# Turning the feed-forward x in place on VectorE, with its blocks regrouped through DRAM

## The chip, the cores and the metric

One core of one Trainium2 chip runs the whole program. The metric is device time in microseconds, the median of several executions. The engines are TensorE (matrix products; PE in the profile), VectorE (DVE), ScalarE (ACT), GpSimd (POOL) and SyncE (SP), which issues the DMAs here. Each engine works through its own instruction list in order and waits on semaphores.

## The reference

The input x has 8192 tokens of 512 numbers (8192x512, f32). What is computed:

```
mod = silu(c) @ wmod                       -> sa, ca, ga, sb, cb, gb   (512 each; ga, gb kept at least 0.25 from 0)
h = layernorm(x) * (1 + ca) + sa
x = x + ga * (causal linear attention of h, 16 heads of 32, then @ W_out + b_out)
h = layernorm(x) * (1 + cb) + sb
g = h @ (w_gate/127).T ;  u = h @ (w_up/127).T          (1536 hidden units)
x = x + gb * ((silu(g) * u) @ (w_down/127).T)
```

The weights w_gate, w_up and w_down are integers from -127 to 127. The result must be accurate to f32, so each f32 operand is split into a rounded high part and a low remainder (float32r), and products are taken with both.

## The kernel before, in words

The program has two parts that follow each other. The attention part takes 16 groups of 512 tokens. The feed-forward part takes 8 groups of 1024 tokens (FG = 8; group G, token tiles of 128, halves of 512 tokens) and runs from about 1012 us to the end. Its loop over G is written once in a hardware loop for the middle groups, and once each for the first and the last.

**Steps.** The hidden units are taken in 12 blocks of 128 (HB = 12; block q). For each block TensorE computes gate and up for both token halves with a Winograd scheme of seven products, p1 to p7, each of four matmuls 128x512 (`product`, line 1868). A step on TensorE is p1(q), p7(q-1), p2(q), p5(q), p4(q-1), p6(q), p3(q). The other engines work beside it:

- ACT (`step` in `scalar`) saves PSUM banks and takes the silu: save_p1 (line 1573), save_p5 (1568), silu1 (1583), h_high (1595), save_u2 (1578), h_high, then a place for something extra, silu2 (1590).
- VectorE (`step` in `vector`) adds and multiplies: add_c22(q-1) (line 1715), add_c11(q) (1704), times_gate2(q-1) (1729), times_gate1(q-1) (1721), a place for something extra (`aside`), add_c12(q) (1710).
- GpSimd computes the low parts of the hidden values, h_low (line 1497), and adds the residual (1502).

The waits around this are: p6(q) for add_c11(q), p5(q) for add_c12(q-1), p4(q-1) for add_c22(q-1), p7(q) for save_u2(q), which is behind silu1(q) on ACT; silu1(q) waits for times_gate1(q-1), and that for p4(q-1).

**Down rows.** After steps 5 and 11 comes a half of the down projection: eight token tiles (`down`, line 1925), each twelve matmuls, into four PSUM banks in turn. VectorE multiplies each by gb (`gate_y`, line 1736), GpSimd adds the residual that SP has loaded (`load_residual`, line 1411), SP stores it (`store`, 1428). A bank's next row waits for the gate_y of the row four before.

**The next group's x.** While group G runs, the tiles of group G+1 (loaded by `load_x`, line 1405, into eight tiles of 128x512: the four of xg and four of z_exp and z_relu) get their layer norm on VectorE: `norm_stats` (1681) in steps 2 to 5, `norm_var` in step 5, `rstd_of` on GpSimd, `norm_x` (1697) behind the first half and in steps 7 to 9. They have tokens on the partitions, and the products need features there. So TensorE turns them: `turn` (line 1936) makes four 128x128 transposes into a PSUM bank, eight times a group: behind steps 8 to 11, and four between the first down rows of the second half. ACT brings each bank to SBUF with scale and shift, `evacuate` (line 1562), one each in the extra place of steps 9 to 11, one after step 11 and four later.

**Behind step 11** VectorE makes the operands of the next group's products from these: the Winograd sums T1 to T4 (`sum_of`, 1671) and low parts (`low`, 1675) for both k, with ACT's high parts (`high`, 1547) between, and the second half's gate_y among them in a fixed order that ends with add_c11 of the next group, for which p6 of the next group waits:

```python
            sum_of(G + 1, T1, 0)
            sum_of(G + 1, T2, 0)
            add_c22(G, 11)
            sum_of(G + 1, T3, 0)
            times_gate2(G, 11)
            low(G + 1, T1, 0)
            times_gate1(G, 11)
```

**The SP queue** issues, in order, the loads of the weight parts for block q+4 (`load_parts`, line 1393, 1 MB, each waiting for p4 of the block that used its place), and after each six of them the stores and residual loads of a half; `load_x` stands among the second half's.

**End of the attention part.** The first feed-forward group's x is turned in the attention part. Its two halves are loaded into xg by one DMA each (line 404) in the last two attention groups; VectorE's `norm_stats` there (line 757) waits for them, and stands ahead of the gating and dividing of the attention tiles, for which TensorE waits.

Of the kernel before, what the change touches and what calls it, by code (L numbers as in the profile page):

```python
# [43 lines left out]
Shared = namedtuple("Shared", "xg xf h_hi h_lo ring b_hi b_lo full wd silu_sum saved gate h y x_res gb_row pairs sums dn")  # L44
# [24 lines left out]
def build(nc, x, w_qkv, b_qkv, b_cols, w_out, b_out, c_vec, c_row, w_mod, w_mod_t, ffn_words, out):  # L69
    top = ExitStack()  # L70
    with top:
# [10 lines left out]
        k_dram = nc.dram_tensor("k_dram", (P, D), F32, kind="Internal").ap()  # L82
        gb_dram = nc.dram_tensor("gb_dram", (1, D), F32, kind="Internal").ap()
# [60 lines left out]
        ffn = feed_forward(sem, later, ident, mod_col, half_neg, norm, gb_dram, parts, att, shared, x_mid, out)  # L144
# [40 lines left out]
def attention(nc, s, sem, sbuf, psum, ident, gb_dram, mod_col, half_neg, w_hi, w_lo, xt_hi, xt_lo, ga_row,  # L185
# [5 lines left out]
    z_exp = sbuf(s, "z_exp", [P, 2, GN])  # L191
    z_relu = sbuf(s, "z_relu", [P, 2, GN])
# [40 lines left out]
    v_ready, ksum_ready, prod_ready, prod_turned = sem("v_ready"), sem("ksum_ready"), sem("prod_ready"), sem("prod_turned")  # L233
# [26 lines left out]
    shared = Shared([xg[:, t, :] for t in range(GT)] + [z[:, i, :] for z in (z_exp, z_relu) for i in range(2)],  # L260
# [42 lines left out]
    def sync(sp, first_loads):  # L303
# [449 lines left out]
    def vector(dve, sum_of, low):  # L753
        def norm_stats(g, tiles=range(GT)):
            wait(dve, x_in, 16 * (g + 1))
# [568 lines left out]
def feed_forward(sem, later, ident, mod_col, half_neg, norm, gb_dram, parts, att, shared, x_mid, out):  # L1324

    stats, mean_var, var_eps, rstd = norm[1:5]
    xg, xf, h_hi, h_lo, (blocks, filled), b_hi, b_lo, full, wd, total, saved, gate, h, y, x_res, gb_row, xs, sums, dn = shared
# [8 lines left out]
    xt_ps, xf_ready = sem("fxt_ps"), sem("fxf_ready")  # L1336
    gb_in, gb_chain, gb_done = sem("gb_in"), sem("gb_chain"), sem("gb_done")
# [50 lines left out]
    def sync(sp):  # L1388
# [7 lines left out]
        def load_x(G):  # L1396
            if isinstance(G, int) and G == 1:
                sp.wait_ge(att.xt_ps, (NG + 2) * C)
            else:
                wait(sp, xt_ps, (G - 1) * 8)  # L1400
# [83 lines left out]
    def gpsimd(pool):  # L1484
# [24 lines left out]
        def body(G):  # L1509
            ahead = not isinstance(G, int) or G + 1 < FG  # L1510
            for q in range(HB):
                if q not in (5, 11):
                    h_low(G, q, 1)
                    h_low(G, q, 0)
                if q == 5:
                    h_low(G, q, 1)
                    h_low(G, q, 0)
                    if ahead:
                        rstd_of(G + 1)
# [18 lines left out]
    def scalar(act):  # L1538
# [10 lines left out]
        def evacuate(G, i, bank):  # L1549

            k, which = divmod(i, 4)
            c = (k, k + 2, k, k + 2)[which]
            wait(act, xt_ps, G * 8 + (i - 7))
# [8 lines left out]
            act.activation(to, bank, ACT.Identity, bias=mod_col[:, SB, c:c + 1],  # L1562
# [47 lines left out]
        def body(G):  # L1610
# [12 lines left out]
            for q in range(7, HB):  # L1623
                step(G, q, (lambda i=q - 9: evacuate(G + 1, i, dn[i])) if ahead and q >= 9 else nothing)
# [4 lines left out]
            evacuate(G + 1, 3, dn[3])  # L1629
# [7 lines left out]
            for i, bank in ((4, sums[0]), (5, sums[1]), (6, xs[0]), (7, xs[1])):  # L1637
                evacuate(G + 1, i, bank)
# [20 lines left out]
    def vector(dve):  # L1659
# [39 lines left out]

        def add_c11(G, q):  # L1700
# [54 lines left out]
        def step(G, q, extra, last_tile):  # L1755
            add_c22(G, q - 1)
            if isinstance(G, int) and G == 0 and q == 1:
                last_tile()
            add_c11(G, q)
            times_gate2(G, q - 1)  # L1760
            times_gate1(G, q - 1)
            extra()
            add_c12(G, q)

        def body(G, last_tile):
            ahead = not isinstance(G, int) or G + 1 < FG

            def aside(q):
# [19 lines left out]
            times_gate1(G, 5)  # L1788
            for i in range(FT - 1):
# [271 lines left out]
```

## Time and profile before

| | |
|---|---|
| time, median of 3 runs (lowest, highest) | 1996.83 us (1996.74, 1998.13) |
| the profiled execution: its time | 1998.45 us |
| its span, first to last instruction | 1996.7 us |
| TensorE's mean granted clock, share of full | 0.998 |
| one group of the feed-forward part (1298.54 to 1423.20) | 124.7 us |

A row of a timeline gives the start, the time taken (of all instructions merged into it), the engine, the line of the kernel, the operation, output and inputs by tile name with their shape, and in brackets how long the engine stood before it and what released it. Some names are shared, since tiles are reused: `k_tok` and `kv_diag` are ACT's saved banks, `r_den` is c11 or c12, `bv_row` is c22, `y_rows` the gated hidden values, `sc`, `pj`, `num` and `state` PSUM banks, `full` and `xf` the turned x and its sums.

### The profile page before, as it was taken

The numbers are of one execution on the slowest core, as the hardware profiler recorded it, in microseconds if no ns is written. First come the engines' busy times: TensorE is split into PE (matmuls) and PEld (weight loads), VectorE is DVE, ScalarE is ACT, GpSimd is POOL, SyncE is SP. The second block draws the span as 40 slices with busy tenths as digits, with TensorE's granted clock in tenths as the row PEclk, the third lists the DMA queues.
The fourth block names the chain that finished last, engine by engine and source line by source line (L and its number), as shares of the span: only waits on it lengthen the run. The fifth ranks groups of instructions, "written<-read, shape, count | busy, mean of one in ns | idle before, by whom it ended". The sixth has DMA issues, their size and how long they took to land. (4 is left out here: it accounts for less than half of the span.)

```text
span 1996.7 us, 43856 instructions
## 1 busy us (share of the span) xinstructions
PE 1960.6 (98%) x16008; PEld 1591.9 (80%) x16008; DVE 1443.1 (72%) x2386; ACT 905.7 (45%) x1542; POOL 877.4 (44%) x718
## 2 busy tenths in 40 slices
PE   7999999999999999999899999999999999999999
PEld 4788888888888888887678888788888888888887
DVE  7977888878788878787865857658576585765744
ACT  5443444344444434443344535445354453544533
POOL 2533544444544444453334443444434444344444
PEclk9999999999999999999999999999999999999999
DMA  7223333444434434432575654656546565465553
GB/s 268 69 91 102 115 123 119 135 130 133 135 100 133 128 125 135 127 110 90 179 263 176 207 187 145 214 170 209 186 144 215 171 210 186 144 214 174 169 168 106
DMA packets 202521, 309.81 MB, mean 155 GB/s; under 512 B 16145, under 2 KB 72977, under 8 KB 202386
## 3 DMA queue, kind: packets, MB, share of 16 engines
q1 hardware_dynamic: 201858, 306.78, 48.1%
q8 instruction: 107, 1.75, 0.4%
q10 hardware_dynamic: 528, 1.05, 0.1%
q14 instruction: 28, 0.23, 0.0%
HBM read 225.19 MB, written 82.58 MB: 154 GB/s over the span
## 5 line engine op out<-in xcount | busy, mean ns | idle before, releaser
L1497 POOL TENSOR_TENSOR h_lo<-y_rows,h_hi 128x512 fp32r<-128x512 f32 x192 | 246.5, 1301 | 367.6 <-ACT h_hi L1595 367.6
L461 POOL TENSOR_TENSOR x_res<-y,x_res 128x512 f32<-128x512 f32 x64 | 86.6, 1353 | 294.0 <-DVE y L872 283.5
L851 DVE TENSOR_TENSOR probs<-sc,causal 128x512 f32<-128x512 f32 x256 | 158.5, 681 | 3.8 <-PE sc L1156 2.6
L612 ACT ACTIVATE z_exp<-pj,qk_neg 128x512 f32<-128x512 f32 x128 | 87.7, 686 | 161.5 <-PE pj L1137 158.0
L1137 PE MATMUL pj<-xt_hi,w_hi 128*128 128x512 f32 x512 | 145.9, 406 | 5.7 <-DVE a_t L861 4.7
L1925 PE MATMUL sc<-wd,h_hi 128*128 128x512 f32 x384 | 150.7, 392 | 0.0
L1925 PE MATMUL sc<-wd,h_lo 128*128 128x512 f32 x384 | 149.6, 389 | 0.0
L450 POOL TENSOR_TENSOR a_lo<-a_t,a_hi 128x512 fp32r<-128x512 f32 x60 | 82.2, 1370 | 144.8 <-ACT a_hi L626 144.8
L1137 PE MATMUL pj<-xt_lo,w_hi 128*128 128x512 f32 x512 | 138.1, 391 | 1.8 <-DVE xt_lo L789 1.8
L1137 PE MATMUL pj<-xt_hi,w_lo 128*128 128x512 f32 x512 | 138.1, 392 | 0.0
L1710 DVE TENSOR_TENSOR r_den<-pj,k_tok 128x512 f32<-128x512 f32 x96 | 66.3, 691 | 97.9 <-ACT k_tok L1578 52.2
L1595 ACT ACTIVATE h_hi<-y_rows 128x512 fp32r<-128x512 f32 x192 | 119.0, 620 | 24.9 <-DVE y_rows L1729 13.4
L1573 ACT ACTIVATE k_tok<-sc 128x512 f32<-128x512 f32 x96 | 56.2, 585 | 158.7 <-PE sc L1868 158.7
L445 POOL TENSOR_TENSOR prod<-k_sum,qt 128x512 f32<-128x512 f32 x64 | 94.1, 1471 | 61.4 <-DVE qt L797 42.5
L597 ACT ACTIVATE xf<-sc,mod_col 128x512 f32<-128x512 f32 x64 | 49.8, 778 | 152.7 <-PE sc L1097 152.7
L1137 PEld LDWEIGHTS pj<-xt_hi,w_hi 128*128 128x128 f32 x512 | 91.8, 189 | 33.1 <-DVE a_t L861 11.0
L1137 PEld LDWEIGHTS pj<-xt_lo,w_hi 128*128 128x128 f32 x512 | 96.2, 188 | 23.3 <-DVE xt_lo L789 2.2
L1568 ACT ACTIVATE kv_diag<-pj 128x512 f32<-128x512 f32 x96 | 57.4, 598 | 123.9 <-PE pj L1868 122.9
L1137 PEld LDWEIGHTS pj<-xt_hi,w_lo 128*128 128x128 f32 x512 | 96.7, 189 | 20.9
L1583 ACT ACTIVATE k_sum<-r_den 128x512 f32<-128x512 f32 x96 | 60.7, 632 | 107.7 <-DVE y_rows L1721 95.0
L1721 DVE TENSOR_TENSOR y_rows<-sc,k_sum 128x512 f32<-128x512 f32 x96 | 66.3, 691 | 55.6 <-PE sc L1868 55.6
L1715 DVE TENSOR_TENSOR bv_row<-sc,kv_diag 128x512 f32<-128x512 f32 x96 | 66.3, 691 | 54.8 <-PE sc L1868 54.8
(248 smaller groups left out, 5390.4 us busy)
## 6 DMA issues: line engine op xcount, KB each, us to landing
w_hi<-parts SPq DMA_DIRECT2D x48, 1024.0 KB, 5.4
w_lo<-parts SPq DMA_DIRECT2D x48, 1024.0 KB, 5.4
x_mid<-x_res SPq DMA_DIRECT2D x96, 256.0 KB, 2.8
x_res<-in_L_attn_x SPq DMA_DIRECT2D x64, 256.0 KB, 2.8
k_dram<-k_block SPq DMA_DIRECT2D x252, 64.0 KB
xg<-in_L_attn_x SPq DMA_DIRECT2D x15, 1024.0 KB, 7.4
x_res<-x_mid SPq DMA_DIRECT2D x60, 256.0 KB, 3.9
full<-x_mid SPq DMA_DIRECT2D x60, 256.0 KB, 3.7
```

The costliest lines, as they stand in the source:

```text
L445: pool.tensor_tensor(out=prod[:, c % 2, :], in0=k_sum[:, c % 2, :], in1=qt[parity][:, c, :], op=ALU.mult).then_inc(prod_ready, 1)
L450: pool.tensor_tensor(out=a_lo[:, :], in0=a_t[:, :], in1=a_hi[:, :].bitcast(F32), op=ALU.subtract).then_inc(a_lo_ready, 1)
L461: pool.tensor_tensor(out=x_res[:, slot, :], in0=y[:, :], in1=x_res[:, slot, :], op=ALU.add).then_inc(y_ready, 1)
L612: act.activation(z_exp[:, n % 2, :], pj[:, n % 2, :], ACT.Relu, bias=qk_neg[:, 1 - kind, c:c + 1], scale=-scale).then_inc(below_ready, 1)
L851: dve.tensor_tensor(out=probs[:, h, :].rearrange("p (c i) -> p c i", c=C), in0=sc[:, h, :].rearrange("p (c i) -> p c i", c=C), in1=causal[ ...
L1137: mm = pe.matmul(to, w[:, k, at:at + P], xt[:, k, :], start=(i == 0), stop=(i == len(passes) - 1))
L1497: pool.tensor_tensor(out=h_lo[b], in0=h[i], in1=h_hi[b].bitcast(F32), op=ALU.subtract).then_inc(h_lo_ready, 1)
L1595: act.activation(h_hi[q % 6 * 2 + i], h[i], ACT.Copy).then_inc(h_hi_ready, 1)
L1710: dve.tensor_tensor(out=c12, in0=sums[1], in1=s12, op=ALU.add).then_inc(c12_ready, 1)
L1715: dve.tensor_tensor(out=c22, in0=xs[q % 2], in1=s5, op=ALU.add).then_inc(c22_ready, 1)
L1721: dve.tensor_tensor(out=h[0], in0=xs[q % 2], in1=gate[0], op=ALU.mult).then_inc(h1_ready, 1)
L1925: mm = pe.matmul(dn[i % 4], as_(part[j * 2 + t // GT][:, rows]), as_(wd[half * 6 + j]), start=(j == 0 and part is h_hi), stop=(j == 5 and ...
```

## The change

- TensorE's `turn` is taken out, with its waits. In its place VectorE's `turn` transposes a 128x512 tile in place, in blocks of 32x32, which leaves features and tokens in the right order only within a block.
- The blocks are therefore put in place by DMA ahead of it: after the layer norm, `save_xn` stores a half's four tiles to DRAM (`xn_dram`), and `load_blocks` loads them back so that partition block h holds columns h*128 to h*128+127, 32 tokens each (four DMAs of 256 KB in pieces of 512 bytes).
- The eight transposes stand singly among VectorE's instructions of steps 10 and 11. ACT's `evacuate` reads the turned tiles from SBUF by a strided pattern instead of PSUM: evac 0 and 1 in step 11's extra place, 2 and 3 right behind, 4 to 7 where they were.
- `norm_stats` and `norm_var` move one step ahead (not for the first group), `norm_x` to behind the first half and between its gated rows. `rstd_of` moves with them.
- add_c22 of block 11 moves ahead of T1 and T2.
- Since features now come in another order (head slices regrouped), w_gate, w_up and the sb and cb rows of wmod are reordered on the host, and the two loads of line 404 become sixteen DMAs each, whose source pieces are 32 numbers (128 bytes).

```diff
+        z = sbuf(s, "z", [P, 4, GN])        # was z_exp and z_relu
...
-                sp.dma_start(xg[:, :, :], mid_groups[half, :, :, :]).then_inc(x_in, 16)
+                for t in range(GT):
+                    for c in range(C):
+                        sp.dma_start(xg[:, t, c * P:(c + 1) * P].rearrange("p (h e) -> p h e", h=HPC),
+                                     mid_groups[half, :, t, :].rearrange("p (h c e) -> c p h e", h=HPC, c=C)[c]
+                                     ).then_inc(x_in, 16)
...
+        def save_xn(G, second):
+            wait(sp, xn_ready, G * 4 + (2 * second - 2))
+            sp.dma_start(xn_dram[second * GN:(second + 1) * GN, :].rearrange("(t p) d -> p t d", p=P),
+                         xg_halves[second][:, :, :]).then_inc(xn_out[second], 16)
+
+        def load_blocks(G, second):
+            wait(sp, xn_out[second], G * 16)
+            for h in range(HPC):
+                sp.dma_start(xg_halves[second][h * E:(h + 1) * E, :, :].rearrange("p t (b x) -> p (t b) x", x=P),
+                             xn_dram[second * GN:(second + 1) * GN, h * P:(h + 1) * P].rearrange("(b i) x -> i b x", i=E)
+                             ).then_inc(xb_in[second], 16)
...
                     if not last or q + 4 < HB:
                         load_parts(G, q + 4)
+                    if not last and q in (5, 6):
+                        save_xn(G + 1, q - 5)
+                    if not last and q in (7, 8):
+                        load_blocks(G + 1, q - 7)
...
-        def evacuate(G, i, bank):
+        def evacuate(G, i):
...
-            wait(act, xt_ps, G * 8 + (i - 7))
+            c, second = (k, k + 2, k, k + 2)[which], which // 2
+            wait(act, xt_ps, G * 8 + (4 * second - 4))
...
-            act.activation(to, bank, ACT.Identity, bias=mod_col[:, SB, c:c + 1],
+            turned = xg_halves[second][:, :, :].rearrange("p t (b c i) -> p c (t b) i", c=C, i=E)[:, c, :, :]
+            act.activation(to.rearrange("p (b i) -> p b i", i=E), turned, ACT.Identity, bias=mod_col[:, SB, c:c + 1],
...
-                step(G, q, (lambda i=q - 9: evacuate(G + 1, i, dn[i])) if ahead and q >= 9 else nothing)
+                step(G, q, (lambda: (evacuate(G + 1, 0), evacuate(G + 1, 1))) if ahead and q == 11 else nothing)
...
-            evacuate(G + 1, 3, dn[3])
+            evacuate(G + 1, 2)
+            evacuate(G + 1, 3)
...
+        def turn(G, t):
+            wait(dve, xb_in[t // GT], G * (16 * HPC))
+            dve.transpose(xg[t], xg[t]).then_inc(xt_ps, 1)
...
             add_c22(G, q - 1)
...
+            turning = q >= 10 and (not isinstance(G, int) or G + 1 < FG)
+            first = (q - 10) * GT
+            if turning:
+                turn(G + 1, first)
             add_c11(G, q)
             times_gate2(G, q - 1)
+            if turning:
+                turn(G + 1, first + 1)
             times_gate1(G, q - 1)
             extra()
+            if turning:
+                turn(G + 1, first + 2)
             add_c12(G, q)
+            if turning:
+                turn(G + 1, first + 3)
...
-                if ahead and not first and 2 <= q < 6:
-                    norm_stats(G + 1, q - 2)
-                if ahead and q == 5:
+                if ahead and not first and 1 <= q < 5:
+                    norm_stats(G + 1, q - 1)
+                if ahead and q == (5 if first else 4):
                     norm_var(G + 1)
-                if ahead and 7 <= q < 10:
-                    norm_x(G + 1, q - 6)
...
             times_gate1(G, 5)
+            if ahead:
+                norm_x(G + 1, 0)
+                norm_x(G + 1, 1)
             for i in range(FT - 1):
                 gate_y(G, i)
+                if ahead and i in (3, 4):
+                    norm_x(G + 1, i - 1)
...
+            add_c22(G, 11)
             sum_of(G + 1, T1, 0)
             sum_of(G + 1, T2, 0)
-            add_c22(G, 11)
...
-        def turn(G, i, bank):
-            k, which = divmod(i, 4)
-            c, second = (k, k + 2, k, k + 2)[which], which // 2
-            wait(pe, xn_ready, G * 4 + (2 * second - 2))
-            for t in range(GT):
-                mm = pe.transpose(bank[:, t * P:(t + 1) * P], xg[second * GT + t][:, c * P:(c + 1) * P], ident[:, :])
-            mm.then_inc(xt_ps, 1)
```

## Rows read from the trace of the kernel before

**Rows 1.** Busy time, share of the span and instructions of TensorE, whole execution.

```profile
PE 1960.6 (98%) x16008; PEld 1591.9 (80%) x16008; DVE 1443.1 (72%) x2386; ACT 905.7 (45%) x1542; POOL 877.4 (44%) x718
```

**Rows 2.** Waits of TensorE's weight loads, 1012 to 1997: us in total, times, longest.

```profile
PEld sc L1868 <- ACT k_tok L1578: 12.1, 42, 0.7
PEld sc L1925 <- DVE a_t L1736: 1.5, 7, 0.2
```

**Rows 3.** Timeline of TensorE around the turn behind step 8.

```profile
1450.89 0.62 PE L1868 MATMUL pj<-xt_hi,w_hi 128*128 128x512 f32 x2
1451.35 0.60 PE L1936 MATMUL num<-ident,xg 128*128 128x128 f32 x4
1451.70 0.71 PE L1868 MATMUL sc<-w_hi,w_lo 128*128 128x512 f32 x2
1452.25 0.63 PE L1868 MATMUL sc<-xt_hi,w_lo 128*128 128x512 f32 x2
```

**Rows 4.** Timeline of VectorE: times_gate1(9), times_gate1(10), T1, T2, add_c22(11).

```profile
1463.50 0.69 DVE L1721 TENSOR_TENSOR y_rows<-sc,k_sum 128x512 f32<-128x512 f32 x1 [0.61 <-PE sc L1868]
...
1470.34 0.69 DVE L1721 TENSOR_TENSOR y_rows<-sc,k_sum 128x512 f32<-128x512 f32 x1 [0.61 <-PE sc L1868]
...
1473.98 1.47 DVE L1671 TENSOR_TENSOR full<-xf 128x512 f32<-128x512 f32 x1 [0.44 <-ACT xf L1562]
1475.49 0.69 DVE L1671 TENSOR_TENSOR full<-r_den,full 128x512 f32<-128x512 f32 x1
1476.10 0.68 DVE L1715 TENSOR_TENSOR bv_row<-sc,kv_diag 128x512 f32<-128x512 f32 x1
```

**Rows 5.** Timeline of all engines where the next group begins; then VectorE in its steps.

```profile
1499.84 0.68 DVE L1704 TENSOR_TENSOR r_den<-pj,k_tok 128x512 f32<-128x512 f32 x1
...
1500.64 0.30 PEld L1868 LDWEIGHTS sc<-w_lo,w_hi 128*128 128x128 f32 x2 [0.25 <-issue]
...
1513.90 0.69 DVE L1721 TENSOR_TENSOR y_rows<-sc,k_sum 128x512 f32<-128x512 f32 x1 [0.62 <-PE sc L1868]
...
1517.61 0.69 DVE L1715 TENSOR_TENSOR bv_row<-sc,kv_diag 128x512 f32<-128x512 f32 x1 [0.51 <-PE sc L1868]
...
1520.44 0.69 DVE L1721 TENSOR_TENSOR y_rows<-sc,k_sum 128x512 f32<-128x512 f32 x1 [0.62 <-PE sc L1868]
```

**Rows 6.** Timeline of ACT in step 11: evac 2 and silu2(11).

```profile
1473.18 0.77 ACT L1562 ACTIVATE xf<-sc,mod_col 128x512 f32<-128x512 f32 x1
1473.84 0.63 ACT L1590 ACTIVATE gabo_row<-r_den 128x512 f32<-128x512 f32 x1
```

**Rows 7.** Timeline of GpSimd: both h_low of block 10.

```profile
1472.35 2.55 POOL L1497 TENSOR_TENSOR h_lo<-y_rows,h_hi 128x512 fp32r<-128x512 f32 x2 [4.29 <-ACT h_hi L1595]
```

**Rows 8.** Line 845, attention's transposes on VectorE: min/median/max ns, first and last start.

```profile
L845 DVE STREAM_TRANSPOSE k_block<-kt x63: 662/670/714, 63.4 to 972.8; 128x512 f32<-128x512 f32 x63
```

**Rows 9.** Timeline of SP's issues: the two loads of line 404.

```profile
895.78 0.39 SPq L404 DMA_DIRECT2D xg<-x_mid  x1
...
956.47 0.39 SPq L404 DMA_DIRECT2D xg<-x_mid  x1
```

**Rows 10.** Timeline of VectorE, bn_stats of the first of these loads.

```profile
908.02 1.86 DVE L757 BATCH_NORM_STATS2 stats<-xg 128x6 f32<-128x512 f32 x3
```

**Rows 11.** Timeline of VectorE in the last attention group, from the second bn_stats.

```profile
962.17 1.29 DVE L757 BATCH_NORM_STATS2 stats<-xg 128x6 f32<-128x512 f32 x2 [0.45 <-DMA xg<-x_mid]
963.63 0.69 DVE L872 TENSOR_TENSOR y<-pj,ga_row 128x512 f32<-128x512 f32 x1 [0.18 <-PE pj L1206]
965.28 0.42 DVE L861 TENSOR_TENSOR a_t<-num,r_den 128x256 f32<-128x256 f32 x1 [0.96 <-PE pj L1181]
```

**Rows 12.** Timeline of TensorE there.

```profile
968.60 1.20 PE L1206 MATMUL pj<-w_hi,a_hi 128*128 128x512 f32 x4 [1.98 <-DVE a_lo L782]
```

**Rows 13.** Stretches: us, busy of PE PEld DVE ACT POOL, PEclk, DMA share, GB/s.

```profile
920.10:923.00 2.90, 2.90 (x21) 2.13 (x25) 1.19 (x3) 1.78 (x3) 1.29 (x1) 1.00 0.36 96
...
956.40:961.70 5.30, 4.47 (x33) 3.34 (x26) 4.37 (x7) 2.38 (x5) 3.73 (x3) 1.00 0.96 320
```

More of the change, by code:

```diff
@@ L43 @@
 Signals = namedtuple("Signals", "wide_ready wd_in xt_ps xf_ready a_ready y_gated y_ready y_out xr_ready state_ready op_ready pj_ready part_out b_ready sum_made b_high")
-Shared = namedtuple("Shared", "xg xf h_hi h_lo ring b_hi b_lo full wd silu_sum saved gate h y x_res gb_row pairs sums dn")
+Shared = namedtuple("Shared", "xg xg_halves xf h_hi h_lo ring b_hi b_lo full wd silu_sum saved gate h y x_res gb_row pairs sums dn")
 Turned = namedtuple("Turned", "kt qt v r_den probs prod k_block k_sum a_hi a_lo")
@@ L143, in build @@
                                       x_mid, k_dram, parts, downs)
-        ffn = feed_forward(sem, later, ident, mod_col, half_neg, norm, gb_dram, parts, att, shared, x_mid, out)
+        ffn = feed_forward(sem, later, mod_col, half_neg, norm, gb_dram, parts, att, shared, x_mid, xn_dram, out)
         block = top.enter_context(nc.Block())
@@ L754, in norm_stats @@
         def norm_stats(g, tiles=range(GT)):
-            wait(dve, x_in, 16 * (g + 1))
+            wait(dve, x_in, 16 * (g + 1) if not isinstance(g, int) or g < NG else 16 * (NG + GT * C * (g - NG + 1)))
             for t in tiles:
@@ L1321, in attention, with feed_forward @@
     return Programs(sync, gpsimd, scalar, vector, tensor), signals, shared
-def feed_forward(sem, later, ident, mod_col, half_neg, norm, gb_dram, parts, att, shared, x_mid, out):
+def feed_forward(sem, later, mod_col, half_neg, norm, gb_dram, parts, att, shared, x_mid, xn_dram, out):
     stats, mean_var, var_eps, rstd = norm[1:5]
-    xg, xf, h_hi, h_lo, (blocks, filled), b_hi, b_lo, full, wd, total, saved, gate, h, y, x_res, gb_row, xs, sums, dn = shared
+    xg, xg_halves, xf, h_hi, h_lo, (blocks, filled), b_hi, b_lo, full, wd, total, saved, gate, h, y, x_res, gb_row, xs, sums, dn = shared
     c11, c12, c22 = total
@@ L1336, in feed_forward @@
     xt_ps, xf_ready = sem("fxt_ps"), sem("fxf_ready")
+    xn_out, xb_in = [sem(f"xn_out{i}") for i in range(2)], [sem(f"xb_in{i}") for i in range(2)]
     gb_in, gb_chain, gb_done = sem("gb_in"), sem("gb_chain"), sem("gb_done")
@@ L1399, in load_x @@
             else:
-                wait(sp, xt_ps, (G - 1) * 8)
+                wait(sp, xf_ready, (G - 1) * 8)
             for t in range(FT // 2):
@@ L1511, in body @@
             for q in range(HB):
+                if ahead and q == (5 if isinstance(G, int) and G == 0 else 4):
+                    rstd_of(G + 1)
                 if q not in (5, 11):
@@ L1636, in body @@
             high(G + 1, T4, 0)
-            for i, bank in ((4, sums[0]), (5, sums[1]), (6, xs[0]), (7, xs[1])):
-                evacuate(G + 1, i, bank)
+            for i in range(4, 8):
+                evacuate(G + 1, i)
             for op in (B11, B21, T1, T2, B22, T3, T4):
@@ L1793, in body @@
             add_c12(G, 6)
-            if ahead:
-                norm_x(G + 1, 0)
             for q in range(7, HB):
@@ L1962, in body @@
                     step(G, q)
-                    if ahead and q >= 8:
-                        wait(pe, y_gated, G * 16 + FT)
-                        turn(G + 1, q - 8, dn[q - 8])
                 i = half * FT
-                if half and ahead:
-                    wait(pe, xf_ready, G * 8 + 1)
                 down(G, i, range(4))
                 p7(G, first + 5)
-                if half and ahead:
-                    wait(pe, xf_ready, G * 8 + 2)
                 down(G, i + 1, range(4))
                 p4(G, first + 5)
-                if half and ahead:
-                    wait(pe, c11_ready, G * HB + HB)
-                    turn(G + 1, 4, sums[0])
-                    wait(pe, c12_ready, G * HB + HB)
-                    turn(G + 1, 5, sums[1])
-                    wait(pe, h1_ready, G * HB + (HB - 1))
-                    turn(G + 1, 6, xs[0])
-                    wait(pe, xf_ready, G * 8 + 4)
                 down(G, i + 2, range(4))
-                if half and ahead:
-                    wait(pe, h1_ready, G * HB + HB)
-                    turn(G + 1, 7, xs[1])
                 down(G, i + 3, range(4))
@@ L2021 @@
 _TURNED = ("L0_c",)
+REGROUPED = np.arange(D).reshape(HPC, C, E).transpose(1, 0, 2).reshape(D)
 def word_blocks(w_gate, w_up, w_down):
-    w_gate, w_up = (np.asarray(w).reshape(HB, P, C, P).transpose(0, 2, 3, 1) for w in (w_gate, w_up))
+    w_gate, w_up = (np.asarray(w)[:, REGROUPED].reshape(HB, P, C, P).transpose(0, 2, 3, 1) for w in (w_gate, w_up))
     units = [np.concatenate([w_gate[j, k], w_gate[j, k + 2], w_up[j, k + 2], w_up[j, k]], axis=1)
@@ L2049 @@
         if name == "L0_wmod":
-            layouts.append(("in_wmod_t", a.T))
+            turned = np.ascontiguousarray(a.T).reshape(6, D, D)
+            for m in (SB_MOD, CB_MOD):
+                turned[m] = turned[m, REGROUPED]
+            layouts.append(("in_wmod_t", turned.reshape(6 * D, D)))
         for label, a in layouts:
```

11 lines of the change are left out of this document (4 added, 7 removed).

## The prediction

> **What bounds the kernel now.** I read the busy shares first, then what TensorE's weight loads wait for in the feed-forward part, then the timelines of one group's end, engine by engine, and last the end of the attention part. TensorE is busy for 98% of the span [rows 1], so every TensorE instruction taken away looks like time won. The waits say that it is not so simple: in the eight feed-forward groups TensorE is held 42 times by ACT's saves (12.1 us in all), and once in each of seven groups by a gated output row [rows 2]. These are short, but they show that chains of the other engines already run level with TensorE, and a chain that runs level becomes the bound as soon as TensorE is relieved.
>
> The first chain is a step's: p4(q-1), times_gate1(q-1), silu1(q), h_high, save_u2(q), p7(q). Steps without a turn behind them follow each other every 6.54 us by the starts of times_gate1 (1513.90 to 1520.44) [rows 5]; steps with one every 6.84 us (1463.50 to 1470.34) [rows 4]. The second is VectorE's queue behind step 11: from the sum T1 at 1473.98 [rows 4] to add_c11 of the next group at 1499.84 it works almost without a gap, and p6 of the next group starts only after that, at 1500.65 behind a gap of 0.25 [rows 5]. So at the group's end it is VectorE, not TensorE, that sets the time now. The third is the attention part's last group, where bn_stats starts at 962.17 after a wait for the xg load of line 404 [rows 11] and TensorE then stands 1.98 us for VectorE's a_lo [rows 12].
>
> **Part by part.** *TensorE's turns go.* Four transposes take 1451.35 to 1451.70, and the pair of matmuls behind them takes 0.55 instead of the 0.46 of the pair before them [rows 3]: some 0.45 us a turn, 3.6 us for the eight of a group, 25 us for seven groups. That would be the gain if TensorE alone set the time. But the turns behind steps 8, 9 and 10 lie in the first chain, where taking one away brings a step from 6.84 to 6.54: 0.90 us by the time of times_gate1(10). The turns after step 11 (half of them and one more) lie beside the second chain, which does not get shorter by them: nothing.
>
> *Eight VectorE transposes come in.* A 128x512 stream transpose takes 0.67 us (0.66 to 0.71 in 63 of them) [rows 8]; operations of 0.68 to 0.69 us start 0.61 apart when they are queued (1475.49 to 1476.10) [rows 4], so I take 0.60 from start to start. In step 10 and in step 11 two of them stand between add_c22 and times_gate1. Now times_gate1 starts 2.83 us after add_c22 (1517.61 to 1520.44), with some idle time between [rows 5]; with them the queue is full and it takes three sums and two transposes, 3 x 0.61 + 2 x 0.60 = 3.03. So times_gate1 is 0.20 late, and the whole step chain behind it, twice: 0.40. Bounds 0.17 (some overlap) and 0.42 a step (0.71 each). The other two of each step lie where VectorE waits for save_u2 and p7: nothing. Sum at times_gate1(10): 0.90 - 0.40 = 0.50 us earlier.
>
> *ACT's evacuations move.* Before, one stood in each of steps 9 to 11, and evac 2 at 1473.18, 2.84 us after times_gate1(10), released T1 at 1473.98, 3.64 after it [rows 4, 6]. Now evac 0 and 1 both stand there, then silu2(11), then evac 2. An evacuation takes 0.77 us, and the next instruction starts 0.66 after it [rows 6]; from SBUF it is not in the trace, so I bound its distance by 0.66 and 0.77 and take 0.70, near the row. silu2 lasts 0.63, some 0.54 from start to start by the same overlap. Evac 2 then starts 2.84 + 1.40 + 0.54 = 4.78 after times_gate1(10) and ends 0.80 later; T1 starts at 5.60 instead of 3.64.
>
> *VectorE's queue behind it.* c22(11) now goes ahead into idle time: 0.61 less. T1 took 1.47, since GpSimd's h_low(10) ran from 1472.35 for 2.55 us [rows 7] and a subtraction of two SBUF tiles stood until it was over; T1 comes later now, when h_low(10) is done: about 0.90 less. T2 waits some 0.08 for evac 3. From T1 to add_c11 it was 1499.84 - 1473.98 = 25.86 [rows 4, 5]; it becomes 24.43. So add_c11 of the next group starts 5.60 + 24.43 = 30.03 after times_gate1(10), against 29.50: 0.53 later. With the 0.50 earlier above, a group comes out at +0.03 us, seven groups at +0.2; with both bounds of each term between -0.3 and +0.7 a group, -2 to +5 us.
>
> *norm_stats, norm_var and norm_x move* into idle time of steps 1 to 4 and of the first half's gated rows, where GpSimd's residuals and their loads set the pace. I cost them at nothing; without this cover they cost about 4 us a group. The SP queue gets save_xn and load_blocks behind loads of parts that it already waits for.
>
> *Loads of xg at the end of attention.* One DMA of 1 MB becomes sixteen of 64 KB in 128-byte pieces, 8192 pieces. The trace has no such piece. In 920.10 to 923.00, the four k_block stores (512 pieces of 512 bytes) took 0.36 x 16 x 2.9 = 16.7 us of DMA engine time, 33 ns a piece; in 956.40 to 961.70, 1.70 MB in 2 KB pieces took 0.96 x 16 x 5.3 = 81 us, 98 ns a piece [rows 13]. A straight line through both gives an estimate of 17 ns for 128 bytes, 8192 x 17 / 16 = 8.7 us. The old load took 962.17 - 956.47 = 5.7 us [rows 9, 11], of which 1.05 MB at 320 GB/s are 3.3, so 2.4 are fixed. The new one lands at 956.47 + 8.7 + 2.4 = 967.6, 5.4 us later. VectorE had 0.18 and 0.96 us of waiting in the two operations behind [rows 11]; the rest, 4.3 us, goes through to TensorE, once. Lower bound: SP's sixteen issues at 0.39 [rows 9] and 2.4 land at 965.1, +1.8 us; upper bound: 33 ns a piece, 16.7 + 2.4, landing at 975.6, +12.3. The first of these two loads has room: issued at 895.78, used at 908.02 [rows 9, 10], 12.2 us against 11.1.
>
> That row prices no piece under 512 bytes. [...]
>
> **Sum.** +0.2 for the groups and +4.3 for the load, 4.5 us on an execution of 1998.45 us whose span is 1996.7; the median of the runs is 1996.83, so I forecast 2001.3 us.
>
> **Rivals.** *1. TensorE does set the end* (faster). If VectorE's queue has more give than I think (fewer subtractions that meet GpSimd, evacuations at 0.60), TensorE's relief counts: at most 25 us less, 1976 with the load's price. For it speaks the 98%; against it the gap at 1500.64, which exists with the turns in place. Between lies a partial gain. It decides from 0.7 us less queue per group on (7 x 0.7 = 4.9 cancels the load): 1992 if half of the turns after step 11 (1.0 us a group) were won.
>
> *2. Small pieces are slow.* Each 128-byte piece costs as much as one of 512 bytes, 33 ns, or more: the second load lands at 975.6 (+12.3) and the first one is late too, by 19.1 - 12.2 = 6.9 us at bn_stats: 2009 to 2016. For it: the line above rests on two sizes. Against it: pieces of 512 bytes already cost a third of those of 2 KB.
>
> *3. The blocks come late.* load_blocks of the second half is issued behind 1 MB of parts after p4(8), which is done when times_gate1(8) starts, at 1463.50 - 6.84 = 1456.66 [rows 4]. 1 MB at 320 and 1 MB at 96/0.36 = 267 GB/s [rows 13] take 3.3 + 3.9, with 2.4 fixed 9.6 us: 1466.3. The fifth transpose follows add_c22(10), at about 1470.34 - 2.83 + 0.61 - 0.6 = 1467.5. That is 1.2 us of room, and steps 7 and 8 move 2 MB each in 6.5 us as well, which is 320 GB/s. A wait there holds add_c11(11), behind it p6(11): 7 us for each us of lateness, 2008 at 1 us, 2015 at 2 us.
>
> **Chances.** Forecast (1997 to 2005): 0.50. Rival 1: 0.14. Rival 2: 0.17. Rival 3: 0.19. Runs of this kernel can tell about 0.2% (4 us) from no change, which is 1992.8 to 2000.8. The forecast's lower part and the small end of rival 1 fall inside: faster 0.13, same 0.31, slower 0.56. Range 1994 to 2015.
>
> **What would show it.** Right: no transposes of line 1936 on TensorE; times_gate1 7 to 11 spaced 6.5, 6.5, 6.7, 6.7; T1 some 5.6 us after times_gate1(10); the time taken off TensorE standing there as a gap in the second half's down rows, whose banks wait for VectorE's gated rows; p6 of the next group still behind add_c11; a wait of some 5 us at bn_stats around 962. Wrong: groups shorter by over 1 us with VectorE idle behind step 11, or VectorE waiting for DMA at a transpose.

## The result, and the profile after

The changed kernel takes 2044.99 us, the median of four executions (2039.15 to 2058.86), against 1996.78 us for the kernel before: a ratio of 1.0252, interval 1.0199 to 1.0305. That is above the forecast of 2001.3 us and above its range, which ends at 2015. The profiled execution took 2043.05 us, its span is 2040.9 us, 44.2 us longer than before. TensorE is relieved, as the busy line of the page shows (it answers to [rows 1]), and the span is longer all the same:

```profile
PE 1954.3 (96%) x15784; PEld 1573.5 (77%) x15784; DVE 1477.6 (72%) x2442; ACT 907.1 (44%) x1542; POOL 892.4 (44%) x718
```

Where the time lies is read from the starts of VectorE's times_gate1, twelve in a group: the table has the first of all, and then the mean over seven groups of the distance from the one before (the last two columns are experiments 7 and 14 below).

| times_gate1 | before | after | 7 (2005 us) | 14 (1993 us) |
|---|---|---|---|---|
| (0) of the first group, from the span's start | 1008.20 | 1017.16 | 1006.40 | 1008.87 |
| (8) | 6.84 | 6.52 | 6.52 | 6.52 |
| (9) | 6.84 | 8.73 | 6.73 | 6.73 |
| (10) | 6.84 | 8.72 | 6.69 | 6.69 |
| (11) | 8.18 | 8.81 | 8.80 | 8.78 |
| (0) of the next group | 28.95 | 29.84 | 30.05 | 27.90 |
| one group | 124.72 | 129.71 | 125.89 | 123.69 |

So 9.0 us come at the end of attention and 7 x 4.99 = 34.9 us in the seven groups. In the fourth of them VectorE's timeline, which answers to [rows 4] and the first line of [rows 5], shows times_gate1(8), add_c22(9), the first transpose, times_gate1(9), the fifth transpose, times_gate1(10), T1, times_gate1(11) and add_c11:

```profile
1475.33 0.69 DVE L1752 TENSOR_TENSOR y_rows<-sc,k_sum 128x512 f32<-128x512 f32 x1 [0.62 <-PE sc L1910]
...
1479.03 0.69 DVE L1746 TENSOR_TENSOR bv_row<-sc,kv_diag 128x512 f32<-128x512 f32 x1 [0.50 <-PE sc L1910]
1481.03 0.71 DVE L1729 STREAM_TRANSPOSE xg<-xg 128x512 f32<-128x512 f32 x1 [1.31 <-DMA xg<-xn_dram]
...
1483.46 0.65 DVE L1752 TENSOR_TENSOR y_rows<-sc,k_sum 128x512 f32<-128x512 f32 x1
...
1489.49 0.71 DVE L1729 STREAM_TRANSPOSE z<-z 128x512 f32<-128x512 f32 x1 [1.67 <-DMA z<-xn_dram]
...
1491.91 0.66 DVE L1752 TENSOR_TENSOR y_rows<-sc,k_sum 128x512 f32<-128x512 f32 x1
...
1497.50 0.69 DVE L1697 TENSOR_TENSOR full<-xf 128x512 f32<-128x512 f32 x1 [1.11 <-ACT xf L1587]
...
1500.70 0.69 DVE L1752 TENSOR_TENSOR y_rows<-sc,k_sum 128x512 f32<-128x512 f32 x1
...
1521.69 0.67 DVE L1735 TENSOR_TENSOR r_den<-pj,k_tok 128x512 f32<-128x512 f32 x1
```

The first transpose of each half stands idle until its blocks have landed, in all seven groups; all that comes behind it in VectorE's queue waits too. The view of line 1729 has the sum, 26.8 us:

```profile
  DMA z<-xn_dram: 13.5, 7
  DMA xg<-xn_dram: 13.3, 7
```

TensorE's waits after 1000 us (total, times, longest) show where it reaches TensorE, in the first line, and two waits of the second half's down rows. In the kernel before no matmul of these rows waited for either; only the weight loads waited for a gated row, 1.5 us in all [rows 2]:

```profile
PE sc L1910 <- DVE r_den L1735: 17.4, 14, 2.8
PE num L1967 <- DVE a_t L1767: 12.3, 6, 2.1
PE num L1967 <- POOL h_lo L1521: 11.2, 7, 4.8
```

SP issues the blocks of the first half behind part 11, those of the second behind part 12, and the four of the second half take 5.83 us to issue alone (SP's timeline, the same group):

```profile
1468.69 0.55 SPq L1399 DMA_DIRECT2D w_hi<-parts  x1
1469.35 3.45 SPq L1423 DMA_DIRECT2D xg<-xn_dram  x4
1475.23 0.55 SPq L1399 DMA_DIRECT2D w_hi<-parts  x1
1475.82 5.83 SPq L1423 DMA_DIRECT2D z<-xn_dram  x4
```

At the end of attention the sixteen loads that replace one take SP 12.04 and 11.22 us ([rows 9] had 0.39), and bn_stats waits for them (first and second group, answering to [rows 10, 11]), the second time for 8.30 us; TensorE's wait for a_lo that [rows 12] shows grows from 1.98 us to 7.39 (last line):

```profile
895.01 12.04 SPq L407 DMA_DIRECT2D xg<-x_mid  x16
959.45 11.22 SPq L407 DMA_DIRECT2D xg<-x_mid  x16
```
```profile
909.01 1.88 DVE L762 BATCH_NORM_STATS2 stats<-xg 128x6 f32<-128x512 f32 x3 [1.71 <-DMA xg<-x_mid]
972.49 1.29 DVE L762 BATCH_NORM_STATS2 stats<-xg 128x6 f32<-128x512 f32 x2 [8.30 <-DMA xg<-x_mid]
```
```profile
976.47 2.07 PE L1211 MATMUL pj<-w_hi,a_hi 128*128 128x512 f32 x4 [7.39 <-DVE a_lo L787]
```

### The profile page after: what moved, and what is told of

Same layout as the page of the kernel before. It is cut to its first block and busy times, and to the rows that moved or that the text cites. A ratio compares the mean times of both kernels' runs of the same rounds, so it can differ in the third digit from the quotient of the medians.

```text
span 2040.9 us, 43467 instructions
## 1 busy us (share of the span) xinstructions
PE 1954.3 (96%) x15784; PEld 1573.5 (77%) x15784; DVE 1477.6 (72%) x2442; ACT 907.1 (44%) x1542; POOL 892.4 (44%) x718
## 5 line engine op out<-in xcount | busy, mean ns | idle before, releaser
L1521 POOL TENSOR_TENSOR h_lo<-y_rows,h_hi 128x512 fp32r<-128x512 f32 x192 | 256.0, 1353 | 392.4 <-ACT h_hi L1620 392.4
L617 ACT ACTIVATE z<-pj,qk_neg 128x512 f32<-128x512 f32 x128 | 88.0, 687 | 162.1 <-PE pj L1142 151.9
L1967 PE MATMUL num<-wd,h_hi 128*128 128x512 f32 x192 | 79.8, 416 | 23.5 <-DVE a_t L1767 12.3
```

The lines of the kernel that those rows point to most:

```text
L617: act.activation(z_exp[:, n % 2, :], pj[:, n % 2, :], ACT.Relu, bias=qk_neg[:, 1 - kind, c:c + 1], scale=-scale).then_inc(below_ready, 1)
L1521: pool.tensor_tensor(out=h_lo[b], in0=h[i], in1=h_hi[b].bitcast(F32), op=ALU.subtract).then_inc(h_lo_ready, 1)
L1967: mm = pe.matmul(dn[i % 4], as_(part[j * 2 + t // GT][:, rows]), as_(wd[half * 6 + j]), start=(j == 0 and part is h_hi), stop=(j == 5 and ...
```

## The experiments

My theory from this profile: late blocks cost some 27 us, the loads at the end of attention 9, and the rest, some 8, comes at the end of a group. Each is taken away by itself, then together.

**1. One load at the end of attention.** norm_x of these two groups writes its columns regrouped, one tile further, so that the load can be one again.

```
-                for t in range(GT):
-                    for c in range(C):
-                        sp.dma_start(xg[:, t, c * P:(c + 1) * P]... , mid_groups...[c])
+                sp.dma_start(xg[:, :, :], mid_groups[half, :, :, :]).then_inc(x_in, 16)
```

> The changed kernel, but the two groups loaded at the end of attention come by one load of 2 KB pieces each, as before; the normalisation writes their columns regrouped instead. Theory (the 16 loads of 128-byte pieces cost the end of attention): the waits of 1.71 and 8.30 us at the statistics go, the first feed-forward step comes about 9 us sooner, the seven groups stay as long as they were; about 2036 us. Rival (the end of attention is late for the regrouped columns or another reason, not for the loads): the first feed-forward step stays late, about 2045 us.

Measured: the first times_gate1 of the feed-forward part starts at 1008.22 us, 8.94 sooner. The time was 2041.8 us (ratio 1.0215, 1.0198 to 1.0232) and not 2036: in the profiled execution the waits for blocks were 36.0 us instead of 26.8. The loads are the whole 9 us of their stage, as far as one execution of each kernel shows: over all the kernels here that have one load, this start lies between 1005.9 and 1009.8. That the groups stay as long did not hold (131.16 us instead of 129.71): the lateness of the blocks differs from one execution to the next, and this hides a part of the gain in the total.

**2. The blocks asked for sooner.**

```
+                    if not last and q == 6:
+                        save_xn(G + 1, 1)
+                        load_blocks(G + 1, 0)
+                    if not last and q == 7:
+                        load_blocks(G + 1, 1)
                     if not last or q + 4 < HB:
                         load_parts(G, q + 4)
```

> The changed kernel, but SyncE issues the second save and the first half's blocks ahead of the loads of part 10, and the second half's blocks ahead of the loads of part 11: some 6 us sooner, with the same pieces. Theory (the blocks come late for their place in SyncE's queue): VectorE's waits for them, 26.8 us in seven groups, fall under 3 us, steps 10 and 11 shrink from 8.7 us to about 7, about 2018 us. Rival (the transposes in VectorE's queue and the sums behind them set the steps, and the waits for blocks only stand in front of that): the waits fall, but the time stays over 2035 us.

Measured: 2020.0 us (1.0116, 1.0099 to 1.0132), no wait at a transpose, the distances (9) and (10) 6.78 and 7.35 us. The theory holds; in (10) TensorE now waits 4.8 us in all for part 11, which stands behind the blocks.

**3 to 5. Why they land late.** Three edits of load_blocks at its place in the changed kernel: whole rows to the same 32 partitions, whole rows to all 128, and another order of the four.

```
3:  xg_halves[second][h * E:(h + 1) * E, :, :]  <-  128 whole rows, 8 KB to a partition
4:  xg_halves[second][:, t, :]                  <-  the 128 whole rows of tile t, 2 KB to a partition
5:  for h in (0, 2, 1, 3):                          (was range(HPC))
```

> The changed kernel, but each of the eight loads of blocks brings whole rows, 8 KB to a partition, to the same 32 partitions at the same place in the queue, so the features reach the product in the wrong order (that part of the computation is changed). Theory (many pieces of 512 bytes make the blocks land in 9 to 10 us): they land in about 5 us, the waits of 26.8 us fall under 5 us, about 2020 us. Rival (32 partitions at a time, or what else runs then, makes them slow, not the size of a piece): they still land in 8 us or more and the time stays within 5 us of 2045 us.

> The changed kernel, but each load of blocks brings one tile in whole rows of 2 KB to all 128 partitions instead of a quarter of the partitions; place, bytes and number of loads are the same (the tiles are not regrouped, so that part of the computation is changed). Theory (a load that writes 32 partitions only is slow, whatever its pieces): they land in about 5 us instead of 9 to 10, the transposes' waits fall under 5 us, about 2018 us. Rival (the loads are slow for what the queue moves just before, parts of 1 MB and the save): they land in 8 us or more, the time stays at about 2045 us.

> The changed kernel with the four loads of each half in the order of partitions 0, 64, 32, 96 instead of 0, 32, 64, 96. [...] Rival (each load runs alone on the queues, so that its own 32 partitions limit it in any order): landing and waits stay, 2039 to 2050 us.

Measured, in that order: 2046.5, 2014.9 and 2042.75 us. The pages' lists of DMA issues (KB, median us from issue to landing) of the changed kernel, of 3, of 4 and of 5:

```profile
xg<-xn_dram SPq DMA_DIRECT2D x28, 256.0 KB, 8.9
z<-xn_dram SPq DMA_DIRECT2D x28, 256.0 KB, 10.0
```
```profile
xg<-xn_dram SPq DMA_DIRECT2D x28, 256.0 KB, 8.3
z<-xn_dram SPq DMA_DIRECT2D x28, 256.0 KB, 10.5
```
```profile
xg<-xn_dram SPq DMA_DIRECT2D x28, 256.0 KB, 6.2
z<-xn_dram SPq DMA_DIRECT2D x28, 256.0 KB, 5.6
```
```profile
xg<-xn_dram SPq DMA_DIRECT2D x28, 256.0 KB, 8.5
z<-xn_dram SPq DMA_DIRECT2D x28, 256.0 KB, 9.6
```

The size of the pieces is not the reason (in 3 whole rows to the same 32 partitions land as late, in 8.3 and 10.5 us; its theory fell), nor which load follows which (5: 8.5 and 9.6 us, as its rival had it). That a load writes only 32 partitions is the reason: written to all 128, the same bytes at the same place land in time, in 6.2 and 5.6 us, and no transpose waits. The stretches (us; busy of PE, PEld, DVE, ACT, POOL; PEclk; DMA share; GB/s) from the issue of the second half's blocks on, of the changed kernel and of 4, show the same: the DMA engines are full in both (share 1.15 and 1.21, and 1.00), but move 241 and 217 GB/s, against 336.

```profile
1475.80:1481.70 5.90, 5.90 (x26) 4.35 (x24) 2.27 (x5) 3.88 (x7) 2.56 (x2) 1.00 1.15 241
1481.70:1488.00 6.30, 5.18 (x22) 3.85 (x22) 4.92 (x9) 3.28 (x6) 2.55 (x2) 1.00 1.21 217
```
```profile
1467.40:1473.30 5.90, 5.90 (x27) 4.67 (x26) 3.58 (x7) 3.87 (x7) 2.55 (x2) 1.00 1.00 336
```

That is 0.72 and 0.65 of 336, in stretches that hold loads to 128 partitions too. What makes a load to 32 partitions slow no run here shows.

**6. Both edits together, and 7. the second half's blocks behind part 11.**

```
7:  load_parts(G, q + 4)   ahead of   load_blocks(G + 1, 1)   at q == 7
```

> The changed kernel with both edits: one load for each group at the end of attention, and the blocks asked for earlier. Theory (the two costs add and are of different stages): 2045 less 9 less 26, about 2010 us, and what then stays over the kernel before (some 13 us, 2 us a group) is VectorE's queue and GpSimd's at the end of a group. Rival (the transposes themselves are cheap, and TensorE's turns gone are a gain): not above the kernel before, 1990 to 1997 us.

> The version with both edits (2012 us), with the second half's blocks behind the load of part 11 instead of ahead of it. Theory (ahead of it they delay that part, for which TensorE waits 7.6 us in all in steps 10 and 11): those waits fall under 1 us and step 10 falls from 7.35 to 6.75 us; about 2006 us. Rival (the blocks come late again behind it): waits for blocks come back at the second half, 2012 us or more.

Measured: 2012.1 us (1.0075, 1.0056 to 1.0094), then 2005.1 us (1.0047, 1.0032 to 1.0061), with no wait for blocks or parts in 7; both theories hold (2010 and 2006). 8 us stay over the kernel before, 1.17 us a group (125.89 against 124.72 in the table), in (11) and in the way to the next group.

**8. The transposes left out of 7.** `dve.sem_inc(xt_ps, 1)` stands for `dve.transpose(...)`.

> The version of 2005 us (one load, early blocks, part 11 first), with the eight transposes left out: VectorE signals at their places once the blocks are there (that part of the computation is left out). Theory (the transposes cost 0.2 us each in steps 10 and 11 and nothing more, the rest of the 8 us is TensorE's stand behind them): 2.5 us less, 2002 us or more. Rival (eight times 0.6 us in VectorE's queue set the end of each group): over 10 us less, under 1995 us.

Measured: 2003.05 us. (9) and (10) fall from 6.73 and 6.69 to 6.52, the rest stays ((11) 8.84, next group 29.86). Eight transposes cost 0.4 us a group and no more; the theory holds, and the 8 us are not theirs.

**9 and 10. One gate product sooner, and both of step 11's ahead of the sums.** gate_y(G, 8) goes ahead of the low halves of B11, B21 and T4; in 10 also times_gate2(11) and times_gate1(11) ahead of T1 and T3.

```
 9: for op in (T2, B22, T3): low(G + 1, op, 0)      10:  add_c22(G, 11)
    gate_y(G, FT)                                        times_gate2(G, 11)
    for op in (B11, B21, T4): low(G + 1, op, 0)          sum_of T1, T2; times_gate1(G, 11)
    sum_of(G + 1, T1, 1)                                 sum_of T3; low T1; then as 9
```

> The same, and VectorE's first product of the output gate behind step 11 comes three low halves and a sum earlier, ahead of the low halves of B11, B21 and T4. Theory (TensorE, with its turns gone, now stands 2.0 us in each group for that product, and in three groups of seven its clock falls to half for 3.5 us behind the stand): the stand of 14 us in all falls under 3 us and the clock stays at full, two to three us a group less than without the edit; about 1990 us, below the kernel before. Rival (the low halves moved back by it become late for the next group's first products, or the next product of the gate becomes the wait): the time stays within 4 us of the version without it.

> As the one before, and at step 11's end both gate products come ahead of the sums T1 and T3 and of the first low half, so GpSimd's two subtractions for step 11 start about 1.5 us sooner, before VectorE's low halves. Theory (GpSimd's pair takes 3.5 us beside VectorE's low halves, 2.55 us without, and two low halves take 1.77 us instead of 0.68): the pair falls to about 2.6 us, TensorE's waits for it (0.6 us a group) go; about 4 us less than the one before. Rival (the sums wait for ScalarE's evacuations anyway and the collision only moves to other operations): within 2 us of the one before.

Measured: 2009.1 and 2008.9 us, 4 us more than 7; both theories fell, and the rivals hold (the next product becomes the wait). TensorE's longest wait in 7, and what took its place in 9:

```profile
PE num L1979 <- DVE a_t L1779: 14.4, 7, 2.1
```
```profile
PE sc L1981 <- DVE y L1779: 16.3, 7, 2.4
```

TensorE's stand only moved to the next row's bank. In 10, (11) fell to 7.05 us and the next group rose to 32.13: what VectorE gives ahead it takes behind.

**11 to 14. VectorE's queue in TensorE's order.** On 7, and then one on the other: four gate products where TensorE asks for their banks, then three steps more.

```
11: low T2, B22, T3 (k = 0); gate_y(FT); low B11, B21; gate_y(FT + 1); low T4; T1 (k = 1);
    gate_y(FT + 2); T2, T3, T4; low B11, B21 (k = 1); gate_y(FT + 3); low T1, T2, B22, T3, T4; ...
12: add_c11(G + 1, 0)  ahead of  gate_y(G, FT + 4)
13: turn(G + 1, first + 3)  ahead of  add_c12(G, q);  evacuate(G + 1, 2)  into the place of evac 0 and 1
14: add_c12(G + 1, 0)  ahead of  gate_y(G, FT + 7)
```

> The version with one load, early blocks and part 11 first (2005 us), with VectorE's first four products of the output gate in the second half each placed where TensorE asks for its bank (the first behind four low halves, then one every two operations), the sums and low halves of the second 512 tokens behind them. Theory (TensorE stands 2.0 us in each group for one of these products, and runs at half clock behind the stand in most groups; bringing only the first forward moved the stand to the second): stand and half clock go, the way from the last gate product of one group to the first of the next falls from 30.05 to 28.6 us, where VectorE's queue ends; about 1995 us. Rival (VectorE's queue as a whole sets the end, in whatever order): it stays at 30 us and the time at 2004 us or more.

> The same, and the next group's first sum (c11) comes ahead of the fifth and sixth product of the gate. Theory (with the stands gone that sum at the end of VectorE's queue is what TensorE's first step waits for; 1.2 us sooner is 0.6 to 1.2 us a group): 4 to 8 us less than the one before, about 1989 us, below the kernel before. Rival (TensorE itself or the residuals' bank sets the first step then): within 2 us of the one before.

> The version of 1997.6 us (one load, early blocks, part 11 first, four gate products placed, c11 ahead), with the last transpose of steps 10 and 11 ahead of c12, where VectorE is idle for 1.2 us, and ScalarE's third evacuation ahead of its second gate function. Theory (T1 waits 0.64 us for the third evacuation, and VectorE's queue from there on sets the end of a group): T1 comes some 0.6 us sooner, 4 us in all, about 1993.5 us. Rival (the sum's place is not what the end waits for): within 1.5 us of 1997.6.

> The same, and c12 of the next group's first step comes ahead of the last product of the gate, which waits 0.56 us for GpSimd. Theory (c12 leaves VectorE's queue late, behind the last two gate products, which wait 1.5 us for GpSimd's residuals): 0.6 us or more a group, about 1989 us. Rival (TensorE's third product of that step is what c12 waits for): within 1.5 us of the one before.

Measured: 2000.7 (1.0018, 1.0008 to 1.0028), 1997.6, 1998.6 (both 1.0005, 0.9996 to 1.0015) and 1992.6 us (0.9976, 0.9966 to 0.9986). 11 won 4.4 us of the 10 expected, since a wait for add_c11 (9.0 us in seven groups) took the place of the stand. 12 won 3.1 us, less than its theory's 4 to 8; 13 won nothing that can be told, as its rival had it; 14, which keeps the places of 13, won another 6, as its theory had it. The waits of 14 show no stand for a gated row any more, and its time is 4.4 us under that of the kernel before:

```profile
PE num L1974 <- POOL h_lo L1533: 4.2, 7, 0.6
PE sc L1917 <- DVE xt_hi L1712: 3.5, 7, 0.6
```

**15 and 16. Two parts alone, on the kernel before**: the places of norm_stats, norm_var, rstd_of and norm_x; and add_c22(11) ahead of T1 and T2 (both as in the change's diff).

> The kernel before, with the change's places for the statistics, the variance, the power and the normalisation alone; TensorE still turns. Theory (VectorE's idle time in steps 1 to 6 hides them): 1997 us, within 1.5 us of the kernel before. Rival (they make the first half's gate products or GpSimd's low halves late): over 2 us slower.

> The kernel before, with the last c22 ahead of the sums T1 and T2 alone; TensorE still turns. Theory (the two sums come 0.6 us later in a queue that sets nothing there): within 1.5 us of the kernel before. Rival (VectorE's queue from T1 to the next group's first sum sets the end of a group, so 0.6 us a group shows): about 4 us slower, or faster by as much if c22 was what came late.

Measured: 1995.65 us (0.9996, 0.9986 to 1.0005), nothing, as the theory had it; and 2000.1 us (1.0015, 1.0006 to 1.0025), 3.1 us more. In 16 (11) grew from 8.18 to 8.70 us and a group from 124.72 to 125.16: the theory fell, and the rival's size is nearly reached, 0.44 us a group instead of 0.6.

**17. Number or pieces at the end of attention.** The sixteen loads of the changed kernel in 512-byte pieces.

```
-  sp.dma_start(xg[:, t, c * P:(c + 1) * P].rearrange(...), mid_groups[...].rearrange(...)[c])
+  sp.dma_start(xg[:, t, c * P:(c + 1) * P], mid_groups[half, :, t, c * P:(c + 1) * P])
```

> The changed kernel, but the 16 loads of 64 KB of each of the two groups at the end of attention come in pieces of 512 bytes instead of 128 (their columns are not regrouped, so that part of the computation is changed). Theory (a load of 512 pieces of 128 bytes to every 128 partitions takes SyncE 0.72 us to issue, and the size of the pieces sets it): the 16 issues take 6 us instead of 12, the statistics' waits of 10 us in all fall under 3 us, the first feed-forward step comes 6 us or more sooner. Rival (their number sets it, whatever the pieces): the issues still take 11 us or more and the first step stays at 1016 to 1017 us.

Measured: 2036.4 us; the first feed-forward times_gate1 at 1011.18, 6.0 us sooner than with 128-byte pieces and 3.0 later than with one load. SP still needs 8.77 us for the second sixteen, and bn_stats waits 5.78:

```profile
956.31 8.77 SPq L407 DMA_DIRECT2D xg<-x_mid  x16
```
```profile
967.33 1.29 DVE L760 BATCH_NORM_STATS2 stats<-xg 128x6 f32<-128x512 f32 x2 [5.78 <-DMA xg<-x_mid]
```

So of the 9.0 us, some 3 come from the number of loads and some 6 from the pieces, with the scatter of that start named under 1. The issues took 8.5 and 8.8 us, between the theory's 6 and the rival's 11, so each was right in part. Why the size of the pieces counts no run here shows.

## Why the prediction was wrong, by its own steps

*Right.* A turn taken off a step is 0.3 us: 6.52 against 6.84. The transposes cost 0.21 and 0.17 us in steps 10 and 11, forecast 0.20 (7 against 8). T1 starts 5.59 us after times_gate1(10), forecast 5.60; from T1 to add_c11 it is 24.2 us, forecast 24.43 (1521.69 - 1497.50). The moves of the normalisation cost nothing (15).

*Wrong: the blocks, priced at nothing.* "The SP queue gets save_xn and load_blocks behind loads of parts that it already waits for" is the step that failed, and rival 3 was mis-sized. It let the 2 MB land 9.6 us after p4(8), the blocks at 267 GB/s, and only for the second half. That rate came from the k_block stores: they take 32 partitions each too (line 319 of the kernel before), but they read SBUF and do not write it, and their DMA engines were busy for 0.36 of the stretch. In the group shown the fifth transpose starts at 1489.49, 14.2 us after times_gate1(8) (1475.33): the load writes 32 partitions at a time (3 to 5), and the two stretches of the changed kernel above move 2.8 MB (5.9 x 241 + 6.3 x 217), not 2. The first half is late too. Seven groups with 26.8 us of waits are what 2 undoes (25 us); "7 us for each us of lateness" was right, the lateness was 1.9 us, twice. VectorE waiting for DMA at a transpose, the prediction's own sign of being wrong, is there 14 times.

*Wrong: the loads at the end of attention, 4.3 us.* They cost 9.0. I priced the pieces on the DMA engines and sixteen issues at 0.39 us each; the issues took 0.70 to 0.75, so the last was out 11.2 us after the first, and bn_stats started at 972.49 instead of 967.6. The first load, which I gave room, held bn_stats for 1.71 us. That is near rival 2 in time (it let the second load land at 975.6), but by another road: the issues, of which both the number and the pieces count (17).

*Wrong: the group's end, +0.03 us.* With the blocks in time it is +1.17 (7). I took add_c11 for the last of the group's end, by a gap of 0.25 us [rows 5], and TensorE's time without turns for slack. VectorE's queue came out as forecast; but TensorE, some 2 us early, stands 1.07 us for h_lo and 2.05 for the first gated row's bank, and in three of the seven groups its clock then falls to half (in the group shown some 0.6 us behind the second stand); in a fourth, the last, it stands 4.79 us for h_lo and the clock falls within that stand. TensorE's timeline behind step 11 of the group shown, and its stretches (columns as above):

```profile
1504.88 0.50 PE L1967 MATMUL num<-wd,h_hi 128*128 128x512 f32 x1 [1.07 <-POOL h_lo L1521]
...
1506.61 0.39 PE L1967 MATMUL state<-wd,h_lo 128*128 128x512 f32 x1
1509.04 0.50 PE L1967 MATMUL num<-wd,h_hi 128*128 128x512 f32 x1 [2.05 <-DVE a_t L1767]
1509.38 0.39 PE L1967 MATMUL num<-wd,h_lo 128*128 128x512 f32 x1
...
1510.38 0.63 PE L1967 MATMUL num<-wd,h_hi 128*128 128x512 f32 x1
```
```profile
1508.00:1510.00 2.00, 0.96 (x4) 0.77 (x5) 2.00 (x4) 1.01 (x2) 0.85 (x1) 0.92 0.00 0
1510.00:1512.00 2.00, 2.00 (x6) 1.61 (x5) 2.00 (x4) 1.38 (x4) 2.00 (x2) 0.50 0.00 0
1512.00:1514.00 2.00, 2.00 (x8) 1.54 (x7) 2.00 (x2) 0.55 (x1) 1.02 (x1) 0.72 0.82 264
```

The granted clock is 0.50 in the middle stretch, and a matmul takes 0.63 us instead of 0.39. From add_c11 to the next times_gate1(0) it is then 9.24 us instead of 7.5, so TensorE, not add_c11, is last. I had named the gap as a sign that I was right; with the clock behind it, it was the new bound.

It is the half clock that costs, more than the stands. In the first three groups of the changed kernel the stands are as long (1.04 to 1.14 and 2.05 us), but the clock stays at 1.00, as the same stretch of the second group shows:

```profile
1255.20:1257.20 2.00, 2.00 (x10) 1.63 (x9) 2.00 (x4) 1.37 (x4) 2.00 (x2) 1.00 0.00 0
```

In these three the way from times_gate1(11) to the next group's first is 28.62 to 28.63 us (28.76 to 29.33 in the kernel before); in the fourth to the sixth, with half the clock, it is 30.21 to 30.23. In 7 it is 28.94 us in the one group without half clock and 30.22 to 30.25 in the other six, which is nearly all of the 1.17 us a group. Why the clock falls behind the same stands in some groups and not in others stays open.

9 to 14 agree: the stands go only with all four products in TensorE's order, and with the sums ahead too a group falls from 125.89 to 123.69 us, 2.2 us.

*Sum.* 9.0 + 27 + 8 = 44 us, the growth of the span; the 8 is what the groups' 34.9 us leave behind the 26.8, and 7 measures the same. The range let each rival come alone; two came together, with the group's end besides.

## What to carry to other kernels

Price a DMA by the partitions it writes (here 8.3 to 10.5 us to 32, 5.6 to 6.2 to 128) and by its place behind the megabytes ahead of it, not by bytes and a rate from a store in a stretch that was mostly idle; and count what each issue takes of the queue that issues it (0.70 to 0.75 us each, sixteen in a row). Work taken off an engine pays only if the engine that frees its next buffer is reordered with it: else the time becomes a stand, and the clock may fall with it, as it did to 0.50 in four of seven groups here. When a chain comes out as forecast and the time doesn't, look for what has become last behind it.

## What the hardware showed that I had not expected

- At the same place in the queue loads of 256 KB to 32 partitions landed in 8.3 to 10.5 us (medians), whether in pieces of 512 bytes or 8 KB; to 128 partitions, in pieces of 2 KB, in 5.6 to 6.2.
- SP took 0.72 us in the mean to issue a load of 64 KB in 128-byte pieces and 0.54 in 512-byte pieces, sixteen in a row; each of the two of 1 MB in 2 KB pieces took 0.39 in the kernel before [rows 9], 2.11 and 0.39 in 1.
- The sum T4 and the low halves run beside GpSimd's pair of h_low(11), and one side takes longer: in the group shown the pair takes 3.54 us, where that of block 10 took 2.55 in the kernel before [rows 7], and two low halves take 1.80 and 1.75 us instead of 0.68; in the seventh group the eight VectorE operations that start beside the pair all take 0.69 us and the pair 7.27, for which TensorE waits 4.8 us (both lines from GpSimd's timeline). Why they slow each other, and now the one and now the other, no run here shows.

```profile
1501.29 3.54 POOL L1521 TENSOR_TENSOR h_lo<-y_rows,h_hi 128x512 fp32r<-128x512 f32 x2 [4.84 <-ACT h_hi L1620]
...
1893.40 7.27 POOL L1521 TENSOR_TENSOR h_lo<-y_rows,h_hi 128x512 fp32r<-128x512 f32 x2 [4.84 <-ACT h_hi L1620]
```
